# SyncE issues the stores and the loads of a displaced 5x5 convolution from one program and one queue

## What is computed

```python
x = x + _L0_conv_ref(_gn(x), L0_conv_offset)
```

## Time and profile before

| | us |
|---|---|
| median of three runs | 1179.55 |
| the profiled execution, its own time | 1179.43 |
| its span in the trace | 1177.6 |
| PE busy | 1158.7 (98%) |
| POOL busy | 972.2 (83%) |
| DVE busy | 952.8 (81%) |
| ACT busy, its DMA issues not counted | 787.4 (67%) |
| moved by the DMA engines | 402.93 MB, mean 342 GB/s |

### The profile page before, as it was taken

One profiled execution on the slowest core, in us unless ns is written; L12 is line 12 of the kernel. 1 busy time (PEld: TensorE's weight loads), 2 busy tenths in 40 slices (PEclk: granted clock), 3 DMA queues, 4 the chain that ended last, 5 costly groups with the idle time before them and its releaser, 6 DMA issues.

```text
span 1177.6 us, 114501 instructions
## 1 busy us (share of the span) xinstructions
PE 1158.7 (98%) x50736; PEld 1131.0 (96%) x50736; DVE 952.8 (81%) x1373; ACT 787.4 (67%) x873; POOL 972.2 (83%) x1743
## 2 busy tenths in 40 slices
PE   9899999999999999999999999999999999999997
PEld 9899999999999999999999999999999999999997
DVE  6688888878888888888878888888888888888863
ACT  3576776767666676676766666676666767667664
POOL 6678888888888888888888888888888888888884
PEclk9999999999999999999999999999999999999999
DMA  8499999999999999999999999999999999999966
GB/s 270 156 383 378 368 360 363 355 351 357 353 358 359 351 355 356 354 354 355 359 346 358 364 343 360 346 360 359 344 356 354 355 352 357 358 349 359 351 207 212
DMA packets 409760, 402.93 MB, mean 342 GB/s; under 512 B 16528, under 2 KB 409744, under 8 KB 409744
## 3 DMA queue, kind: packets, MB, share of 16 engines
q1 hardware_dynamic: 204944, 201.41, 52.1%
q10 hardware_dynamic: 204800, 201.36, 49.3%
HBM read 201.38 MB, written 201.33 MB: 342 GB/s over the span
## 4 chain that ended last, share of the span: by engine, by line
PE 89%; POOL 5%; issue 2%; POOLq 0%; DVE 0%; DVEq 0%
PE ps L697 59%; PE ps L708 29%; PE ps L689 2%; POOL ay L264 1%; POOL rstd L310 1%; POOL summands L284 0%; POOL summands L286 0%; POOL spread L306 0%; POOL inner L303 0%; POOL var L308 0%; POOL minus_mean L302 0%; POOL mean_sq L301 0%; POOL bias L312 0%; DVE xin L510 0%; POOL norm L326 0%
## 5 line engine op out<-in xcount | busy, mean ns | idle before, releaser
L697 PE MATMUL ps<-ay,norm 32*128 32x128 f32 x24608 | 756.0, 274 | 1.0 <-DVEq L570 1.0
L697 PEld LDWEIGHTS ps<-ay,norm 32*128 32x128 f32 x24608 | 716.0, 187 | 9.7 <-ACTq L676 1.1
L482 DVE BATCH_NORM_STATS2 stats<-xin 128x6 f32<-128x512 f32 x768 | 488.4, 692 | 1.8 <-DMA xin<-in_x_dram 1.8
L621 ACT ACTIVATE y<-ps 128x1536 f32<-128x1536 f32 (+1 forms) x256 | 329.9, 1289 | 157.4 <-PE ps L697 157.2
L708 PE MATMUL ps<-ax,y 64*64 64x64 f32 x24576 | 389.5, 219 | 2.8 <-issue 2.6
L708 PEld LDWEIGHTS ps<-ax,y 64*64 64x64 f32 x24576 | 371.7, 135 | 18.5 <-issue 3.2
L326 POOL TENSOR_SCALAR norm<-xin,rstd,bias 128x768 f32<-128x768 f32 x256 | 293.2, 1145 | 104.5 <-PE ps L697 87.0
L510 DVE TENSOR_TENSOR xin<-ps,xin 128x1024 f32<-128x1024 f32 x256 | 313.2, 1223 | 77.5 <-PE ps L708 76.5
L610 ACT ACTIVATE norm<-xin,bias,rstd 128x768 f32<-128x768 f32 x256 | 262.8, 1027 | 160.4 <-DVE xin L510 84.3
L317 POOL TENSOR_TENSOR xin<-x,xin 128x512 f32<-128x512 f32 x256 | 321.1, 1276 | 7.8 <-ACT x L638 7.7
L638 ACT ACTIVATE x<-ps 128x512 f32<-128x512 f32 x256 | 150.7, 589 | 50.4 <-PE ps L708 50.4
(11 more groups left out here) (62 smaller groups left out, 291.4 us busy)
## 6 DMA issues: line engine op xcount, KB each, us to landing
xin<-in_x_dram SPq DMA_DIRECT2D x512, 384.0 KB, 6.7
out_dram<-xin ACTq DMA_DIRECT2D x512, 384.0 KB, 6.5
off<-in_L_conv_offset_dram SPq DMA_DIRECT2D x1, 48.0 KB, 3.3
```

Source lines behind the costliest of these rows:

```text
L482: nc.vector.bn_stats(stats[:, s // PAIR % RING, s % PAIR, n, :], xin[:, s].rearrange("p (g q) f -> p q f g", g=GROUPS)[:, n]).then_inc(bn_ ...
L621: nc.scalar.activation(y[:, v].rearrange("p k r a m -> p a (k r) m")[:, 0:lanes], ps[:, v, 0:lanes, 0:POS * P].rearrange("p a (n m) -> p a ...
L697: last = nc.tensor.matmul(ps[:, v, a, P * k:P * (k + 1)], norm[rows, v, r, P * k:P * (k + 1)], ay[rows, k, r, :], start=(r == 0), stop=(r ...
```

## The change

ScalarE no longer issues stores. SyncE issues both: in step `s` it waits for the result of step `s` (both parts), issues its two stores, then waits until the store of two steps before has landed and issues the two loads of the next superblock into that slot. The wait on `result1_ready` and the one on `result0_ready` are each followed by an increment of a new semaphore, `store_begun`, for which nothing waits. The first ten slots, the wait for `y_done` and the next six slots stay as they were ahead of all that. Line numbers in the new kernel are higher by 18 in the part behind it.

```diff
         @block.sync
         def _(sync):
+            nc_engine[0] = sync
...
                 load(0, s)
-            with sync.Fori(1, NSUPER) as c:
-                for s in range(SLOTS):
-                    sync.wait_ge(stored[s], 16 * B * c)
-                    load(c, s)
+
+            def store(c, s, t):
+
+                sync.wait_ge(result1_ready, SPARE + t + 1)
+                sync.sem_inc(store_begun, 1)
+                sync.wait_ge(result0_ready, t + 1)
+                sync.sem_inc(store_begun, 1)
+                for b in range(B):
+                    sync.dma_start(out_t[s, b, c], xin[b:P:B, s]).then_inc(stored[s], 16)
+
+            def step(c, s, head, tail):
+
+                store(c, s, STEPS * c + s)
+                if s >= BEHIND and not tail:
+                    sync.wait_ge(stored[s - BEHIND], 16 * B * (c + 1))
+                    load(c + 1, s - BEHIND)
+                if s < BEHIND and not head:
+                    sync.wait_ge(stored[s - BEHIND + STEPS], 16 * B * c)
+                    load(c, s - BEHIND + STEPS)
+            run(step)
...
-            def store(c, s, t):
-                act.wait_ge(result0_ready, t + 1)
-                act.wait_ge(result1_ready, SPARE + t + 1)
-                for b in range(B):
-                    act.dma_start(out_t[s, b, c], xin[b:P:B, s]).then_inc(stored[s], 16)
-
             def step(c, s, head, tail):
...
-                if s >= BEHIND:
-                    store(c, s - BEHIND, t - BEHIND)
-                elif not head:
-                    store(c - 1, s - BEHIND + STEPS, t - BEHIND)
...
-            for s in range(STEPS - BEHIND, STEPS):
-                store(NSUPER - 1, s, TOTAL - STEPS + s)
```

More of the change, by code:

```diff
@@ L133, in displaced_conv @@
         off_loaded = sem("off_loaded")
+        store_begun = sem("store_begun")
         bn_done = sem("bn_done")
```

## The result

The changed kernel takes 1208.22 us (median of four runs, 1207.95 to 1209.19), the kernel before in the same comparison 1179.62 us. The ratio is 1.024, 95% interval 1.0226 to 1.0255: slower by 28.6 us. Predicted were 1194.3 us, with 1182 to 1214 as the range of the likeliest case. The profiled execution took 1208.26 us, its span 1206.5.

The account below looks back on a forecast made before the run. PE was taken to set the pace (98% busy), with DMA close behind. The profiled 1179.4 us plus 14.9 us lateness of the last load, nothing for start and end, gave 1194.3 us; range 1176.5 to 1214, likeliest case 1182 to 1214.

Parts of the forecast that it names:

- the rate R: GB/s of SyncE's single queue alternating two stores and two loads: taken as 347, between bounds 341 and 383.
- What bounds the kernel; the need of 355 against what one queue moves: In the middle PE sets the pace, needing 355 GB/s; one queue was seen to move 341 to 350, two 383.
- The sum: 383.8 MB through SyncE's queue at 347 GB/s: last load lands at 1153.8, due 1138.9, so 14.9 us late.
- at each moment the queue moves in one direction: Reason for 347 GB/s in one queue: harmonic mean of 350 for loads alone and 344 for stores alone.
- The queue doesn't run dry: SyncE's queue always has work: a pair gives eight transfers, 9.1 us of work, each 8.77 us.
- Issues off ScalarE gain nothing; issues onto SyncE cost nothing by themselves: Moving 512 issues, 315 us, off ScalarE changes nothing for PE; SyncE's four per step take 2.4 of 4.4 us.
- Head: At the start, the late load of slot 11 lands sooner: 1.0 us less on PE, lost again in the likeliest case.
- Tail: At the end, the last stores go when their result is ready: 0.4 us at most, nothing in the likeliest case.
- The signs: Profile after: GB/s about 347, DMA share 1.05 to 1.1, DVE waits from step 40 to 100, last load issued 30 us later.
- The rival of the queue that doesn't matter: One queue moves as much as two, so from 351.7 GB/s nothing is late: 1178.0 us; chance 0.38.
- The rival of the bubbles: Changes of direction in the queue leave bubbles: at 330 GB/s late by 71.8 us, 1251 us in all; chance 0.07.
- ScalarE's freedom: Where superblocks meet, freed ScalarE saves PE some tenths per border over 15 borders: 1176 us; chance 0.05.

Follow-up runs that it names:

- x1: The changed kernel with the stores issued by ScalarE on its own queue again, SyncE keeping its new program and waits: 1180.28 us.
- x3: The changed kernel with stores that write only three of the six rows of a slot, same issues, order and waits: 1175.87 us.
- c1: All arithmetic left out; SyncE alone loads and stores every slot on one queue, in the changed kernel's order: 1058.62 us.
- x4: The changed kernel with the four transfers of a step in the order store, load, store, load: 1202.43 us.
- c4: c1 beside TensorE running unused matmuls from a long loop (384 matmuls, 88 times): 1221.14 us.
- c6: Arithmetic left out, loads on SyncE's queue and stores on ScalarE's, beside the long loop of matmuls of c4: 1152.63 us.
- x5: The changed kernel with four stores and then four loads per pair of steps: 1208.93 us.
- x2: The changed kernel on two queues, SyncE storing and loading image 0 and ScalarE image 1, loads four steps behind: 1208.62 us.
- c3: c1 beside TensorE running unused matmuls from a short loop (8 matmuls, 4224 times), which outlasts the copy: 1888.79 us.

## Why the prediction was right

The time lay in the forecast range and the path of the loss was the forecast one. The reason given for the rate R was wrong, and its value was near by luck.

- *What bounds the kernel; the need of 355 against what one queue moves.* Right. With the stores back on their own queue everything comes back (x1), and with fewer bytes only one load is late, in the head (x3).
- *The sum.* Right in its form; the term R was mis-sized, 347 for a measured 342 to 343 GB/s. With 342.5 the same sum gives a last load at 46.8 + 0.9 + 1120.6 = 1168.3 us, 29.4 us late, 1208.8 in all. The timeline of the changed kernel has DVE's wait for that slot end at 1167.99, from the late group of its statistics:

```profile
1167.99 1.31 DVE L500 BATCH_NORM_STATS2 stats<-xin 128x6 f32<-128x512 f32 x2 [1.62 <-DMA xin<-in_x_dram]
```

  From there to the end of the span are 38.5 us, forecast were 38.7. A per cent of R is worth 11 us, which is why 4.5 GB/s were half of the loss.
- *Why R should be 347: "at each moment the queue moves in one direction".* Wrong reason. The two rows it was taken from are real, but a queue that alternates reaches 385 (c1), and finer alternation changed little (x4). What lowers R is TensorE's work beside it, and it lowers one queue more than two (c4, c6). That the mean of two rows from stretches without steady arithmetic came within 1.3% was luck. "The queue doesn't run dry" was right of SyncE's queue as a whole and not of its parts.
- *Issues off ScalarE gain nothing; issues onto SyncE cost nothing by themselves.* Right: ScalarE's wait on "issue" is gone, and PE has nothing of it; x3 has all issues and no loss. SyncE's issues grew to medians of 986 and 797 ns, but in x3, with half the bytes to store, they are 657 and 660: it is the transfers that hold them up.
- *Head.* Right and a little smaller. The load that was 1.49 us late is 0.16 late, and PE's stall is 0.28 in place of 1.02:

```profile
53.09 1.31 DVE L500 BATCH_NORM_STATS2 stats<-xin 128x6 f32<-128x512 f32 x2 [0.16 <-DMA xin<-in_x_dram]
...
56.38 3.03 PE L714 MATMUL ps<-ax,y 64*64 64x64 f32 x192 [0.28 <-issue]
```

- *Tail.* Right. The last result is there at 1200.9, and the stream ends near 1205.5, 4.6 us later, where it had been 4.9:

```profile
1198.27 2.66 POOL L335 TENSOR_TENSOR xin<-x,xin 128x512 f32<-128x512 f32 x2 [6.10 <-ACT x L656]
1199.63 3.12 SPq L217 DMA_DIRECT2D out_dram<-xin  x4
...
1205.50:1206.00 0.50, 0.00 (x0) 0.00 (x0) 0.00 (x0) 0.00 (x0) 0.00 (x0) 0.50 0.06 19
```

- *The signs.* DVE's waits are steady from 195.7 us on, about step 40, the early end of the forecast. GB/s were 343 for some 347, and the DMA share 1.04, just under its range. The last load was issued at 1160.2, 44 us later and not some 30: the 14.5 us more are those of the sum.
- *The rival of the queue that doesn't matter.* With the DMA engines alone it is nearly right (1058.6 against 1054.4 us), and so is the rule of the Trainium skill, "DMA: Bandwidth & Descriptors", section "Issuing engines are not separate DMA queues", which the prediction weighed. Beside TensorE it is wrong: 321 against 346 GB/s. The measurement decides.
- *The rival of the bubbles* fell with x4 and x5. *ScalarE's freedom* gave nothing; that a ScalarE that is held up does cost PE showed in x2.

**What stays open.** By what TensorE delays a part of the transfers. Its reads of SBUF and its instructions both go with the number of matmuls in c3 and c4, and no run separates them. The Trainium skill, "Runtime: NRT & Kernel Launch", section "Instruction fetch mechanics", says that a sequencer fetches its instructions through a DMA queue of its own, in blocks of 256 instructions, and fetches again on a taken branch only when the target is outside its window. The page of the profile counts 17 packets of the kind "instruction" in the changed kernel, 8 in c4 and 3 in c3, and a loop of 8 matmuls should not need more by that page of the Trainium skill, yet it loses 31 GB/s. Nor is it known why two queues are better off. That c6 has about twice as many transfers under way fits its first 100 us. It doesn't by itself explain the 346 GB/s behind them: while the lag stands still, the late part moves as much as the others do, and if that is always the same engine, it is faster beside two queues than beside one.

## What to carry to other kernels

When the transfers need nearly all that the DMA engines can move, as here 355 of 385 GB/s, and TensorE works beside them, try loads and stores on two queues even if one issuer would have time for all: here the second queue was worth 2.4%. Don't let an engine that TensorE waits for stand waiting for a transfer to land (x2). Take the rate that a queue can keep from a long stretch with the matmuls running, never from the head, the tail or a stretch of 40 us in which a lag may still grow. And price it by the deadline of the last load: bytes up to it, divided by the rate, against the instruction that needs it; here one per cent of the rate was 11 us.

## What the runs showed that was not expected

With one queue, TensorE alone took 8% (36.1 matmul records per us) to 17% (67.7) from transfers that have nothing to do with it, while VectorE, ScalarE and GpSimd together, 96 to 98% busy on tiles of their own, took none. Loads alone (352 GB/s) and stores alone (346) are slower than both in one queue (385). The loss came late: with two queues, 382 GB/s held for 60 us beside the same matmuls, while the last completions fell behind. And the mean share of the 16 DMA engines still looked nearly full, 1.04 for 1.09.
